# Moving transposes, norms, scores and copies in a hand-ordered four-layer kernel on one core

## The reference

```python
x = x + tanh(g_xattn[0]) * L0_xattn(layernorm(x), ctx, ctx)        # autocorrelation of 8 heads, by FFT and top-k
x = x + tanh(g_ffn[0])   * L0_ffn(layernorm(x), W, b, A, B, gate_w, gate_b)   # dense 1024x1024 + low-rank part
x = x + tanh(g_xattn[1]) * L1_xattn(layernorm(x), ctx, ctx, mask, wq, wk, wv, wo)
x = x + tanh(g_ffn[1])   * L1_ffn(layernorm(x), W_base, b_base, enc, coefs, masks)
```

## Time and profile before

| | us |
|---|---|
| median of three runs | 3191.18 |
| profiled execution | 3187.3 |
| span of the profiled execution | 3185.5 |
| TensorE busy | 3099.6 |
| VectorE busy | 1946.9 |
| ScalarE busy | 1135.4 |
| GpSimd busy | 701.4 |

### The profile page before, as it was taken

One profiled execution on the slowest core, in us unless ns is written; L12 is line 12 of the kernel. 1 busy time (PEld: TensorE's weight loads), 2 busy tenths in 40 slices (PEclk: granted clock), 3 DMA queues, 4 the chain that ended last, 5 costly groups with the idle time before them and its releaser, 6 DMA issues.

```text
span 3185.5 us, 42536 instructions
## 1 busy us (share of the span) xinstructions
PE 3099.6 (97%) x15200; PEld 2592.5 (81%) x15200; DVE 1946.9 (61%) x4651; ACT 1135.4 (36%) x2381; POOL 701.4 (22%) x576
## 2 busy tenths in 40 slices
PE   8999999998899899999999999999999999999999
PEld 7888788887678778888788888788888788888887
DVE  4333477777453577778666667666667666666532
ACT  4111466664122244444333333333333333333320
POOL 2422388884212123333100000000000000000131
PEclk9999999999899999999999999999999999999999
DMA  7332422113352567777564454454454455443621
GB/s 239 126 126 93 155 55 74 60 41 136 123 194 104 178 224 237 234 257 244 176 241 165 159 187 163 147 209 166 167 179 161 156 199 171 172 159 119 258 87 59
DMA packets 232877, 509.67 MB, mean 160 GB/s; under 512 B 23180, under 2 KB 58124, under 8 KB 232668
## 3 DMA queue, kind: packets, MB, share of 16 engines
q1 hardware_dynamic: 231516, 504.14, 45.9%
q10 hardware_dynamic: 1152, 2.82, 0.3%
HBM read 364.29 MB, written 142.61 MB: 159 GB/s over the span
## 4 chain that ended last, share of the span: by engine, by line
PE 65%; DVE 3%; issue 1%; ACT 1%; POOL 1%; DMA 0%; SPq 0%; DVEq 0%; POOLq 0%; ACTq 0%
PE PB L208 53%; PE PB L770 8%; PE PB L1302 3%; PE PB L741 1%; PE PB L1216 0%; ACT at_ss L1283 0%; DVE at_st L213 0%; DMA wqd<-at_wql 0%; DVE at_xt L1338 0%; DVE f0xt L794 0%; DVE at_ss L1277 0%; DVE at_ss L1294 0%; POOL at_st L217 0%; DVE at_hl L196 0%; ACT at_xr L219 0%
## 5 line engine op out<-in xcount | busy, mean ns | idle before, releaser
L208 PE MATMUL PB<-at_woh,at_ah 128*128 128x512 f32 x1024 | 411.8, 402 | 3.5 <-POOL at_wol L196 1.8
L208 PE MATMUL PB<-at_hh,at_wqh 128*128 128x512 f32 x1024 | 401.6, 392 | 0.1
L208 PE MATMUL PB<-at_hl,at_wqh 128*128 128x512 f32 x1024 | 401.2, 392 | 0.0
L208 PE MATMUL PB<-at_wol,at_ah 128*128 128x512 f32 x1024 | 400.7, 391 | 0.0
L208 PE MATMUL PB<-at_woh,at_al 128*128 128x512 f32 x1024 | 400.6, 391 | 0.0
L208 PE MATMUL PB<-at_hh,at_wql 128*128 128x512 f32 x1024 | 400.1, 391 | 0.0
L1283 ACT ACTIVATE at_ss<-at_ss,at_sm,at_bs 128x256 f32<-128x256 f32 x512 | 301.4, 590 | 270.4 <-DVE at_sm L1281 270.4
L1250 DVE TENSOR_TENSOR at_t<-PB,at_rt 128x512 f32<-128x512 f32 x128 | 88.5, 691 | 434.3 <-PE PB L208 434.3
L1338 DVE SCALAR_TENSOR_TENSOR at_xt<-PB,gt,at_xt 128x512 f32<-128x512 f32 x256 | 190.7, 746 | 115.2 <-PE PB L208 115.1
L193 ACT ACTIVATE at_ah<-PB 128x512 fp32r<-128x512 f32 x128 | 76.7, 599 | 482.3 <-PE PB L208 482.3
L208 PEld LDWEIGHTS PB<-at_woh,at_ah 128*128 128x128 f32 x1024 | 193.8, 189 | 40.5 <-POOL at_wol L196 2.0
(11 more groups left out here) (278 smaller groups left out, 7208.2 us busy)
## 6 DMA issues: line engine op xcount, KB each, us to landing
at_wqh<-wqd SPq DMA_DIRECT2D x96, 512.0 KB, 3.6
at_wql<-wqd SPq DMA_DIRECT2D x96, 512.0 KB, 4.5
at_woh<-wod SPq DMA_DIRECT2D x48, 1024.0 KB, 5.0
at_wol<-wod SPq DMA_DIRECT2D x48, 1024.0 KB, 7.4
at_rawq<-in_wq SPq DMA_DIRECT2D x32, 512.0 KB, 4.8
wqd<-at_wqh SPq DMA_DIRECT2D x32, 512.0 KB, 6.2
wqd<-at_wql SPq DMA_DIRECT2D x32, 512.0 KB, 6.9
at_rawo<-in_wo SPq DMA_DIRECT2D x32, 512.0 KB, 6.5
```

The costliest lines, as they stand in the source:

```text
L208: e.matmul(o, a, b, start=i == 0, stop=last), *(waits if i == 0 else ()), *w, mark=last)
```

## The change

Only the order of the work changes, but for two things: the zeros in the lower half of `btl` are made by ScalarE (a copy scaled by 0) instead of VectorE, and the subtraction for `btl` covers only the upper 64 rows. Nothing is computed differently.

- Dense layer, first pair: the split of B moves from c = 3 to behind `flip(2)` at c = 6; `flip(3)` stands ahead of `piece(1)`, `norm(4)`, `norm(5)`, `add_bias(2)` and `add_bias(3)` at c = 7.
- The attention's first two norms are written in the middle of t = 8 instead of behind t = 6, and its third in the middle of t = 10 instead of behind t = 8.
- Attention, u < 4: `weigh(u)` ahead of the split of q.
- Last three units of a block: `norm(3)` at w = 30 moves from the end to behind the first `output`; `values` at w = 30 between the two outputs, `flip(2)` to the end; at w = 29 `flip(1)` behind `values`; at w = 31 the second `output` and `weigh` ahead of the two projections.
- First unit of a new block (w = 0): `turn(u - 1)` and the first `output` ahead of `scores(u)` and `project(u + 2)`.

```diff
@@ dense, loop over c
                     add_bias(1)
-                    h = op("scalar", lambda e: e.activation(bts[:, :], btr[:, :], ACT.Copy), *e_btr)
-                    l = op("vector", lambda e: e.tensor_tensor(btl[:, :], btr[:, :], asf(bts[:, :]), ALU.subtract), h)
-                    z = op("vector", lambda e: e.tensor_scalar(btl[64:P, :], btr[64:P, :], 0.0, None, ALU.mult), l)
-                    e_bt += [h, l, z]
...
                 if c == 6:
-                    ahead(2)
+                    flip(2)
+                    h = op("scalar", lambda e: e.activation(bts[:, :], btr[:, :], ACT.Copy), *e_btr)
+                    l = op("vector", lambda e: e.tensor_tensor(btl[0:64, :], btr[0:64, :], asf(bts[0:64, :]), ALU.subtract), h)
+                    z = op("scalar", lambda e: e.activation(btl[64:P, :], btr[64:P, :], ACT.Copy, scale=0.0), *e_btr)
+                    e_bt += [h, l, z]
+                if c == 7:
+                    flip(3)
                     piece(1)
-                if c == 7:
-                    ahead(3)
+                    norm(4)
+                    norm(5)
+                    add_bias(2)
+                    add_bias(3)
...
-                if t == 10:
-                    yield "half"
+                if t in (8, 10):
+                    yield -t
@@ cross_attention, preparation
             fetch_x(0, 3)
-            nq[2] = norm(0, 2)
             yield
             flip(0, 1, 0, nq[1])
             flip(0, 1, 1, nq[1])
+            nq[2] = norm(0, 2)
@@ cross_attention, loop over u
-                if u < NU:
+                new = w == 0 and 0 < u < NU
+                last = w == 31 and more
+                if u < NU and not new:
                     scores(u)
-                last = w == 31 and more
-                rest = project(u + 2) if u + 2 < NU and not late and not last else None
+                rest = project(u + 2) if u + 2 < NU and not (late or last or new) else None
                 if u < 4:
+                    weigh(u)
                     rest()
-                    weigh(u)
                 if 2 <= u <= 4:
                     values(u - 2)
                 if 1 <= u <= NU:
                     turn(u - 1)
                 if rest and u >= 4:
                     rest()
-                if last:
-                    flip(qn + 1, 3, 0, nq[3])
-                    flip(qn + 1, 3, 1, nq[3])
                 if n:
                     output(n - 1, 2 * k)
-                if last:
-                    project(u + 1)()
-                    load_wq(u + 3)
+                if late:
+                    nq[3] = norm(qn + 1, 3)
+                if new:
+                    scores(u)
                     project(u + 2)()
                 if more and w == 29:
                     flip(qn + 1, 0, 0, nq[0])
                     flip(qn + 1, 0, 1, nq[0])
                     fetch_x(qn + 1, 3)
+                if last:
+                    flip(qn + 1, 3, 0, nq[3])
+                    flip(qn + 1, 3, 1, nq[3])
+                if u == NU or late:
+                    values(u - 1)
+                if n:
+                    output(n - 1, 2 * k + 1)
+                if 4 <= u < NU:
+                    weigh(u)
+                if last:
+                    project(u + 1)()
+                    load_wq(u + 3)
+                    project(u + 2)()
+                if 4 <= u < NU and not late:
+                    values(u - 1)
+                if more and w == 29:
+                    flip(qn + 1, 1, 0, nq[1])
+                    flip(qn + 1, 1, 1, nq[1])
                 if late:
                     flip(qn + 1, 2, 0, nq[2])
                     flip(qn + 1, 2, 1, nq[2])
-                if u == NU:
-                    values(u - 1)
-                if n:
-                    output(n - 1, 2 * k + 1)
-                if more and w == 29:
-                    flip(qn + 1, 1, 0, nq[1])
-                    flip(qn + 1, 1, 1, nq[1])
-                if 4 <= u < NU:
-                    weigh(u)
-                if 4 <= u < NU:
-                    values(u - 1)
                 split_ahead(u)
                 if more and w == 27:
                     nq = {t: norm(qn + 1, t) for t in range(2)}
-                if more and w in (29, 30):
-                    nq[w - 27] = norm(qn + 1, w - 27)
+                if more and w == 29:
+                    nq[2] = norm(qn + 1, 2)
@@ driver
-            if t == 6:
+            if t == -8:
                 next(at_)
...
-            if t == "half":
+            if t == -10:
                 next(at_)
```

## The result

| kernel | median of runs, us | runs | profiled execution, us | its span, us |
|---|---|---|---|---|
| before | 3190.27 (3186.57 to 3191.39) | 7 | 3187.3 | 3185.5 |
| after | 3200.59 (3199.12 to 3201.41) | 7 | 3199.81 | 3198.0 |

The ratio is 1.0036, 95% interval 1.0026 to 1.0045: the change makes the kernel slower, by 10.3 us of the medians and 12.5 us of the two spans. The forecast was 3203.0 us and +11.8.

A forecast was written before the change was run, and what follows sets the result against it. TensorE's own instruction order was taken as the bound (97% busy). Terms of -6.3 + 0.7 + 1.3 + 0.8 + 6.3 + 2 x 4.5 gave +11.8 us, 3203.0 us on the 3191.18 median; term bounds 3193.5 to 3208, stated range 3188 to 3209.

The forecast's parts named there:

- The sum: Whole kernel: all terms together make it 11.8 us slower, 3203.0 us on the median.
- First pair: First dense layer: product(2,0) starts at 817.0, 6.3 us gained, with fs standing behind two norms on ScalarE.
- Ports of VectorE and GpSimd: First pair's lower part: 2.58 us taken; under the skill's port rule it would end some 0.6 us later.
- Norms 0 and 1: Dense layer, tile 8: piece(16)'s wait goes, 5.0 us of wait comes at lora_in(10); 0.7 us lost.
- third norm: Dense layer, middle of tile 10: copies of flip(13) start later, delaying lora_in(12); 1.3 us lost.
- Opening of the attention: Units u below 4: weigh ahead of q's split makes q's low half late; 0.8 us lost.
- Changes two and three: Second and third change of block: output(7,0) waits 2.95 us for values(30)'s split; 4.5 us lost at each.
- the early norm: End of a block, w = 30: moving norm(3) forward gains nothing net, +0.2 us.
- Change one: First change of block: output(7,0) waits 5.6 us for the last output weight, then slow clock; 6.3 us lost.
- Rival 1: Block's new opening is covered, so changes of block cost about nothing: 3186 us; chance 0.16.
- rival 2: Changes of block: early norm works as cover and three waits go, some 6 us each: 3170 us; chance 0.07.
- rival 3: First pair gains all 10.5 us that lora_in(2) comes forward: 3199 us; counted inside the forecast's 0.74.

The follow-up runs named there:

- e11: The changed kernel run once more, unchanged, for one execution: 3202.24 us, span 3200.4.
- e5: Kernel before with only the first pair's edit, but norm(4) behind lora_in(2), and norm(5) with both add_bias behind add_lora(1): 3183.60 us, ratio 0.9989.
- e4: Kernel before with the first pair's edit alone: 3183.06 us, ratio 0.9985.
- e3: Changed kernel with both the early norm of w = 30 and the new block's opening undone: 3193.22 us, ratio 1.0013 of before.
- e8: Changed kernel with values(30) moved between the two projections at w = 31: 3195.40 us, ratio 1.0025 of before.
- e10: e9 with e6's change of block, and third and fourth norms right behind the transposes of t = 0 and t = 2: ratio 1.0008 of before.
- e1: Changed kernel with the opening undone, so scores and projection again precede turn and first output: 3194.69 us, ratio 1.0016 of before.
- e2: Changed kernel with the early norm of w = 30 undone (norm(3), values(29), transposes of t = 2 at old places), opening kept: 3198.93 us, ratio 1.0031 of before.
- e9: Kernel before with the first pair's edit, but lora_in(2) and piece(2) ahead of add_lora(0): 3181.70 us, ratio 0.9982.
- e7: Kernel before with only the attention's first three norms moved inside the dense layer, to tiles 8 and 10: ratio 1.0006.
- e6: Kernel before with only the order of w = 31 changed and turn(31) put ahead of scores(32): ratio 1.0006.

## Why the prediction was right, step by step

- **The sum.** The spans give +12.5 for the first trace of after and +14.9 for e11, the forecast +11.8. That it is so near is in part luck, as errors of a microsecond cancel in it.
- **First pair**, -6.3 forecast, -6.17 measured. Errors cancel. `piece(2)` started at 806.59 and not at 805.2, 1.4 us later than I had it: 0.7 because all of this stretch already lay later in this execution, the rest inside it. The matmuls of `piece(3)`, which wait for the next slice, then found TensorE at full clock, 1.98 us against the 3.52 that my 5.05 us from before contain. Counted from `flip(2)` the gain is 6.9. That `fs` behind two norms takes 3.7 of the 10 us is what e5 tested: without it the wait is gone, and a transfer takes its place.
- **Ports of VectorE and GpSimd.** The lower part took 3.36 us, from 793.48 to 796.84, and not 2.58. It ended 1.07 us behind the end of GpSimd's second `add_bias` (795.77), about what one undisturbed split of that width takes (1.23 at 775.44 in before), although it had begun 2.3 us ahead of that end. The Trainium skill (SBUF — State Buffer, Who interferes with whom) has an engine wait for the port pair until the other's instruction is over; the trace agrees. VectorE, then GpSimd, in after, and the same two in e4:
```profile
793.48 3.36 DVE L990 TENSOR_TENSOR f0btl<-f0btr,f0bts 64x1024 fp32r<-64x1024 f32 x1 [0.15 <-ACT f0bts L989]
791.03 4.74 POOL L750 TENSOR_TENSOR f0xt<-f0xt,f0bg 128x1024 f32<-128x1024 f32 x2 [2.40 <-ACT f0bg L873]
```
```profile
793.22 1.22 DVE L990 TENSOR_TENSOR f0btl<-f0btr,f0bts 64x1024 fp32r<-64x1024 f32 x1 [0.15 <-ACT f0bts L989]
790.95 5.74 POOL L750 TENSOR_TENSOR f0xt<-f0xt,f0bg 128x1024 f32<-128x1024 f32 x2 [2.40 <-ACT f0bg L873]
```
  Between these two traces 0.1 us decides who waits. In after the second `add_bias` began at 793.39, just ahead of the subtraction, and took 2.38 us; in e4 it began at 793.30, just behind it, and took 3.39. With the same edit the subtraction took 2.9 to 3.4 us in after, e3, e5, e8, e10 and e11 and 1.2 to 1.4 in e1, e2, e4 and e9. The 0.6 us that I named for the rule would be a cost in the first kind only, and they aren't seen in the end: from the gates' transposes at 779 to `product(2,0)` after takes 37.8 us and e4 37.7, since in e4 VectorE waits 0.84 us for GpSimd's memset in `piece(1)` instead.
- **Norms 0 and 1**, +0.7 forecast: no wait at `piece(16)`, 4.74 us at `lora_in(10)`; **third norm**, +1.3 forecast: 1.24 us at `lora_in(12)`. Together 2.13 in after, 2.05 in e7 (forecast 2.0), 0.9 in e8's trace, where the slow clock behind `lora_in(10)` was shorter.
- **Opening of the attention**, +0.8 forecast, -0.44 measured. The two waits for the low half of q are 0.8 and 0.5 us longer (4.66 and 3.99 instead of 3.88 and 3.51; forecast 0.5 and 0.2 to 0.3), but the slow clock around them lasted less: the granted clock of the stretch is 0.94 instead of 0.92. Over all traces the stretch from the first `scores` to the unit after the opening (1072.77 to 1154.16 in before) takes 80.4 to 82.0 us with the old order (before, e4 to e7, e9, e10; mean 81.4) and 81.0 to 82.9 with the new one (after, e1 to e3, e8, e11; mean 82.3). The difference of the means, 0.9, is the forecast's 0.8; the first trace of after happens to be the lowest of its kind. One trace alone can't show a term of this size.
- **Changes two and three**, +4.5 each forecast, +4.86 and +4.94 measured, +4.9 and +4.0 in e11. `project(32)` starts 44.32 us behind `scores(29)`, which is 2018.45 on the clock of before; forecast 2018.5. `output(7,0)` waits 2.84 (forecast 2.95), and its twelve matmuls take 4.28 instead of 2.88: the slow clock cost 1.4, and I had 1.0. At the third change of e11 the same wait of 2.85 us is followed by the twelve matmuls at full clock, which is why it cost only 4.0.
- **What was wrong in this step** is to whom the cost belongs. I wrote that the early norm gains nothing net, +0.2. e3 shows that moving `flip(3)` and the second output gains 2.1 us up to `project(32)`, and the early norm takes 2.3 again in after (42.02 to 44.32; up to 3.2 in e1): a sum of nearly zero made of two terms that I didn't see. And the second output that moved was the cover of q for head 33: with scores first it would have cost 2.46 us and mostly a slow clock (behind it at all three changes of e3, and at the first of e1). So the two edits belong together: once the output is moved, opening the block with turn and output hides q and exposes `al`; neither cover is free.
- **Change one**, +6.3 forecast, +6.64 measured, and +5.43 in e11. `project(32)` starts 45.63 us behind `scores(29)`, where before needs 44.71 and still has 2.72 of output to do: the gain of 1.8 that I had. `output(7,0)` waits 5.42 us for the last output weight (forecast 5.6). The reason given, its copy standing behind that of `values(30)`, falls with e8: it stands behind q for head 33. The time was the same because in after all three run back to back.
- **Rivals.** Rival 1 (opening covered) is out by the 2.84 and 5.42 us waits; rival 2 (early norm as cover) by the 4.06 us ahead of `values(29)`; rival 3 (first pair keeps all) by 817.16, and the kernels without the norms ahead of `fs` show that `product(2,0)` comes 10.1 us forward in e9 and 11.7 in e10, which has e9's dense layer, and that 7.3 last in both.
- Not in the sum: 0.93 us in the third block, left open, and -0.38 ahead of the first change, where nothing was changed. This last is chance: the stretch from 1149.68 to 1486.38 takes 336.7 us in after, 337.1 in before and 337.1 in e11.

## What to carry to other kernels

A step that is late can only be moved forward if what then stands behind it on each queue was not the late one's cover: write down for every moved instruction what lay between producer and consumer before, on TensorE as well as on the copying engines. An earlier release also starts its DMAs earlier, and on a queue that waits in order a reload that waits for its own store holds up the load that TensorE needs next (e5: 6.0 us). A sum near zero deserves an experiment for each of its parts: here -2.1 and +2.3 stood behind a +0.2.

## What the runs showed of the hardware that I had not expected

**The slow clock is not decided by the length of the wait alone.** The same 48 matmuls of the two projections behind the same wait of 2.22 or 2.23 us ran at full clock in e3 and partly at the lower level in e2 (window of the two projections in e3, then in e2: us, busy of each engine, granted clock, DMA share, GB/s):
```profile
2013.87:2025.04 11.17, 11.17 (x49) 9.26 (x50) 5.19 (x11) 0.63 (x1) 0.00 (x0) 1.00 0.25 95
```
```profile
2021.55:2034.33 12.78, 12.78 (x49) 10.42 (x50) 5.19 (x11) 0.63 (x1) 0.00 (x0) 0.87 0.23 83
```
In e6 both occur in one execution, 11.17 us at the second change, 12.73 at the first and 12.75 at the third. A term for the slow clock is good to about 1.6 us here, which is more than most of the orders tried differ by. At the third change of after and of e11 the twelve matmuls behind the same wait of 2.84 or 2.85 us took 4.42 and 2.84 us, at a granted clock of 0.61 and 1.00. That is also why the early norm, which costs 2.3 us up to `project(32)`, costs only 0.7 from e2 to after: the wait ahead of the projections is 1.48 us there and they stay at full clock.

**The unit of the attention has two paces.** Pieces of the chain that ended last, in after, in blocks two and three (start, us; 66 matmuls):
```profile
1619.02 13.72 PE PB L208 x66
...
2118.31 13.75 PE PB L208 x66
```
A block goes at 14.59 or at 14.63 us a unit from its second unit to its last, about 0.9 us in all. In blocks two to four, before, e3 and e7 have none of the longer, e2, e6 and e9 two each, after the third in both of its traces. The extra 0.03 us is in the matmuls of the two outputs. What sets the pace isn't known, and no run here tells it apart; a comparison of spans carries it, which is why the terms above are taken from intervals and not from spans.
